# Delta-rule layers: 32 tokens of each of four images to a tile, one state step a tile, four tiles at work, the solution in 32x32 tiles

## The reference

```
q, k = softmax(q), softmax(k); beta = sigmoid(beta)   # from one projection of 776 columns
wk    = W k_t
v_new = beta_t * (v_t - wk)
W     = W + v_new k_t^T
out_t = W q_t
```

## Time and profile before

| | |
|---|---|
| runs | 5322.65, 5342.67, 5358.60 us |
| profiled execution, span | 5373.4 us (its own time; its runs' median is 5342.67) |
| TensorE busy | 4530.5 us, 84% |
| VectorE, ScalarE, GpSimd busy | 2972.1, 2152.0, 831.7 us |
| first delta-rule layer | from 331.4 to 1241.0 us |
| second delta-rule layer | from 1614.2 to 2468.5 us |

### The profile page before, as it was taken

The page is one execution under the profiler, slowest core; times in us unless marked ns, Lnnn a source line. Parts: engine busy times, 40 slices in busy tenths (PEclk is TensorE's granted clock), DMA queues, the critical chain, the costliest instruction groups (busy, mean ns, idle before and its releaser), DMA issues. The chain is left out here.

```text
span 5373.4 us, 139944 instructions
## 1 busy us (share of the span) xinstructions
PE 4530.5 (84%) x57100; PEld 2834.8 (53%) x57101; DVE 2972.1 (55%) x5849; ACT 2152.0 (40%) x4091; POOL 831.7 (15%) x2139
## 2 busy tenths in 40 slices
PE   3679898887997888897688886799999999984995
PEld 1237777773436777774355554354454545433663
DVE  3444444453024544454488886488686877852343
ACT  1133223232123333331466664277575766721221
POOL 0000000000000000000355553011111111104012
PEclk7788878798998988898899998899999999985997
DMA  1000000000000000000100000000000000006123
GB/s 42 2 7 3 3 3 3 3 3 18 0 0 9 4 3 3 3 4 3 38 1 1 1 1 0 10 1 1 1 0 1 0 1 1 0 3 217 61 84 101
DMA packets 47552, 85.70 MB, mean 16 GB/s; under 512 B 7121, under 2 KB 38129, under 8 KB 46065
## 3 DMA queue, kind: packets, MB, share of 16 engines
q1 hardware_dynamic: 40944, 61.84, 3.3%
q0 software_dynamic: 6144, 16.79, 1.0%
HBM read 45.05 MB, written 33.55 MB: 15 GB/s over the span
## 5 line engine op out<-in xcount | busy, mean ns | idle before, releaser
L1775 PE MATMUL psum<-hm_ex,hm_mix 128*128 128x512 f32 x1024 | 510.4, 621 | 42.3 <-ACT hm_Aq L1855 38.3
L1841 ACT ACTIVATE hm_ex<-psum,hm_nm 128x1024 f32<-128x1024 f32 x256 | 285.6, 1116 | 299.4 <-DVE hm_nm L1899 299.4
L1775 PEld LDWEIGHTS psum<-hm_ex,hm_mix 128*128 128x128 f32 x1024 | 175.6, 191 | 352.5 <-issue 344.8
L1914 DVE COPY hm_A<-psum 128x1024 f32<-128x1024 f32 x256 | 312.9, 1222 | 51.5 <-PE psum L1784 47.9
L1909 DVE TENSOR_SCALAR_CACHE_REDUCE hm_plus<-hm_Aq,hm_cbcol,hm_sums 128x1024 f32<-128x1024 f32 x256 | 340.5, 1330 | 0.0
L1899 DVE TENSOR_REDUCE hm_nm<-psum 128x1 f32<-128x1024 f32 x256 | 311.0, 1215 | 13.5 <-PE psum L1763 13.5
L1784 PEld LDWEIGHTS psum<-K,hm_Aq 128*128 128x128 f32 x2048 | 236.6, 140 | 150.0 <-issue 145.4
L957 DVE TENSOR_TENSOR fw_M<-fw_M,psum 128x256 f32<-128x256 f32 x256 | 107.8, 421 | 348.1 <-PE psum L728 345.6
L1846 ACT ACTIVATE hm_junk<-hm_Aq 128x1024 f32<-128x1024 f32 x256 | 270.6, 1057 | 30.3
L1763 PE MATMUL psum<-hm_kt,hm_qd 64*32 64x512 f32 x4096 | 280.1, 606 | 0.0
L1321 ACT ACTIVATE pt_signs<-pt_acts,pt_tb 128x1024 f32<-128x1024 f32 (+1 forms) x224 | 227.6, 1018 | 116.1 <-POOL pt_tb L1188 95.0
(11 more groups left out here) (379 smaller groups left out, 9044.6 us busy)
## 6 DMA issues: line engine op xcount, KB each, us to landing
ex_rows_in<-ex_zero SPq DMA_DIRECT2D x2, 5120.0 KB, 24.8
ex_xs<-ex_rows_in SPq DMA_DIRECT2D x80, 128.0 KB
ex_rows_out<-ex_ys SPq DMA_DIRECT2D x80, 128.0 KB, 1.7
ex_w<-in_ex_w SPq DMA_DIRECT2D x2, 4096.0 KB
X<-in_x SPq DMA_DIRECT2D x2, 2048.0 KB, 12.5
out_y<-X SPq DMA_DIRECT2D x2, 2048.0 KB, 9.0
ff_w<-in_ff_w SPq DMA_DIRECT2D x2, 1024.0 KB, 5.8
pt_w_proc<-in_pt_proc SPq DMA_DIRECT2D x1, 2048.0 KB, 7.6
```

The costliest lines, as they stand in the source:

```text
L1775: mm = pe.matmul(bank[4 + c], mix[:, u, :], ex[:, u, 512 * c:512 * c + 512], start=True, stop=True)
L1841: act.activation(ex[:, u, :], flat2(psum[:, 2 * u:2 * u + 2, :]), ACT.Exp, bias=nm[:, u:u + 1], accum_out=rsum[:, u:u + 1]).then_inc(s_ex, 1)
L1914: dve.tensor_copy(A[:, :, :, QT_ * t:QT_ * t + QT_], flat2(psum[:, 6:8, :]).rearrange("p (m g n) -> p m g n", m=MT, g=HEADS)).then_inc(s_a ...
```

## The change

A tile now holds 32 tokens of each of the four images, one image on each quarter of the partitions. The four groups of a tile belong to different images, so the state is held four times (one per image) and takes one step a tile instead of four; it is set to zero once, not per image. Four tiles are at work: tile i is projected, i-1 factored, i-2 solved, i-3 taken through the state. `solve` uses the compact 32x32 blocks directly, in 4 x 8 small matmuls instead of 8 large ones, so nothing is spread any more. `through_state`, `read_state` and `new_state` (with the part within the group) are made of 32x32 matmuls too. The projection is split into two parts with semaphores of their own. The loop runs seven times. The new order of TensorE and VectorE:

```diff
-    for i in range(-1, 4): ... ; with eng.Fori(1, NT // 4 - 1) ... ; for i in range(NT - 4, NT + 2): ...
+    for i in range(4): ... ; with eng.Fori(1, NT // 4) ... ; for i in range(NT, NT + 3): ...
+    LEN = TILE // B
+    tokens = lambda i: H[...].rearrange("p h (b n) -> p h b n", b=B)[:, :, :, bass.ds(i * LEN, LEN)]
 def solve(by, of, sig):
     for n in range(HEADS):
-        mm = pe.matmul(bank[2][:, 64 * n:64 * n + 64], by[:, n, :], of(n), start=True, stop=True)
+        for b in range(4):
+            mm = pe.matmul(bank[2][rows(b), 64 * n:64 * n + 64], by[rows(b), n, :], of(n)[rows(b)],
+                           start=True, stop=True)
+def read_state(a):
+    for c in range(B):
+        for g in range(2):
+            for j in range(4):
+                at = 256 + 64 * (c // 2) + 32 * g
+                mm = pe.matmul(bank[6 + c % 2][rows(j), at:at + 32], M[rows(j), c % 2, c // 2, g, :],
+                               tr[rows(j), a, 1, g, rows(c)], start=(c < 2 and g == 0), stop=False)
+def through_state(a, half):
+    for g in range(2):
+        for c in range(B):
+            for jb in range(2):
+                j = 2 * half + jb
+                at = 32 * (2 * g + half)
+                mm = pe.matmul(bank[6 + jb][rows(c), at:at + 32],
+                               pkt[rows(j), a % 2, P * g + 32 * c:P * g + 32 * c + 32],
+                               M[rows(j), c % 2, c // 2, g, :], start=True, stop=True)
+def new_state(a, half):
+    for c in (2 * half, 2 * half + 1):
+        for g in range(2):
+            for j in range(4):
+                at = 64 * half + 32 * g
+                n = place(g, j)
+                pe.matmul(bank[6 + c % 2][rows(j), 128 + at:160 + at],
+                          kk[rows(c), a, P * g + 32 * j:P * g + 32 * j + 32], U[rows(c), n, :], ...)
+                mm = pe.matmul(bank[6 + c % 2][rows(j), 256 + at:288 + at], U[rows(c), n, :],
+                               qm[rows(c), a, n, :], ...)
+# TensorE, body i (v = i-1, s = i-2, r = i-3), waits in brackets:
+through_state(r, 0)   [pkt(r), state(r-1), output of r-1 copied]
+solve(nt, first) of s [nt, r0]
+project(i, first 512 columns)
+product(l8, l8t) of v ; through_state(r, 1) ; project(i, the rest)
+product(z1, l2) of v ; solve(nt, later) of s ; read_state(r) [U(r)]
+product(z2, l2) of v ; solve(nt, later) of s ; new_state(r, 0)
+product(tt, l2) of v ; new_state(r, 1) ; turn(i) ; turn_keys(s)
+product(z3, loff) of v ; gram(i, 0) [tr] ; solve(z3, given) of v ; gram(i, 1)
+# VectorE, body i:
+lower(v) ; causal(v) ; solution(s, 0) ; less_max(i) ; corrected(r) ; factor(v, 2) ; sums(i)
+solution(s, 1) ; softmax(i) ; solved(s) ; factor(v, 4) ; state(r)
+# ScalarE, body i:
+l2(v) ; exp(i) ; tt(v) ; tr(i) ; pkt(s) ; output of r [state(r) done] ; nt(v) ; r0(v)
-# gone: keep and the state's reset, spread() for intra, z3x, ntx, inside(), six memsets on GpSimd
...
```

More of the change, by code:

```diff
@@ L618, in fast_weight_stage @@
+        bank, psum = k.bank, k.psum
         rows = lambda c: slice(32 * c, 32 * c + 32)
         flat = lambda ap: ap.rearrange("p h j -> p (h j)")
+        place = lambda g, j: 4 * (j % 2) + 2 * g + j // 2
+        tokens = lambda i: H[:, :, :].rearrange("p h (b n) -> p h b n", b=B)[:, :, :, bass.ds(i * LEN, LEN)]
         def bodies(body, eng, start=None):
-            for i in range(-1, 4):
-                body(i, i % 4, i + 1 < NT, i >= 0, i >= 1, i >= 2)
-            with eng.Fori(1, NT // 4 - 1) as j:
+            for i in range(4):
+                body(i, i, True, i >= 1, i >= 2, i >= 3)
+            with eng.Fori(1, NT // 4) as j:
@@ L631, in bodies @@
                 start()
-            for i in range(NT - 4, NT + 2):
-                body(i, i % 4, i + 1 < NT, i < NT, i - 1 < NT, True)
+            for i in range(NT, NT + 3):
+                body(i, i % 4, False, i < NT + 1, i < NT + 2, True)
         def since(i, n):
@@ L657, in _, with fetch, body @@
[L657 to L661, removed]
+                def fetch(i):
+                    pool.tensor_copy(stage[:, :, :].rearrange("p h (b n) -> p h b n", b=B), tokens(i)).then_inc(s_staged, 1)
+                def body(i, a, new, inv, sol, rec):
+                    if inv:
+                        pool.wait_ge(s_bg, i)
+                        if since(i, 2):
+                            pool.wait_ge(s_t, i * 5 - 5)
+                        pool.tensor_tensor(loff[:, :, :], bg[:, :, :], off, ALU.mult).then_inc(s_lo, 1)
+                    if new and not (isinstance(i, int) and i + 1 >= NT):
+                        pool.wait_ge(s_pj1, i + 1)
+                        fetch(i + 1)
@@ L663, in _, with project @@
+                fetch(0)
+                for i in range(4):
+                    body(i, i, True, i >= 1, i >= 2, i >= 3)
+                with pool.Fori(1, NT // 4 - 1) as j:
+                    for a in range(4):
+                        body(j * 4 + a, a, True, True, True, True)
+                for i in range(NT - 4, NT + 1):
+                    body(i, i % 4, i < NT, True, True, True)
             @block.tensor
             def _(pe):
[L665 to L671, removed]
+                def project(i, n, lo, hi, sig):
+                    for h in range(CH):
+                        mm = pe.matmul(bank[n][:, 0:hi - lo], stage[:, h, :], w[:, h, lo:hi],
+                                       start=(h == 0), stop=(h == CH - 1))
+                    mm.then_inc(sig, 1)
@@ L690, in gram @@
                                 at = 96 * (2 * g + half)
-                                mm = pe.matmul(bank[jb][rows(c), at:at + 96], tr[rows(j), a, 2, g, rows(c)],
+                                mm = pe.matmul(bank[3 + jb][rows(c), at:at + 96], tr[rows(j), a, 2, g, rows(c)],
                                                tr[rows(j), a, :, g, rows(c)], start=True, stop=True)
@@ L719, in with_state @@
[L719 to L743, removed]
+                def read_state(a):
[5 more added lines that the diff above has]
+                                               tr[rows(j), a, 1, g, rows(c)], start=(c < 2 and g == 0), stop=False)
+                    mm.then_inc(s_o, 1)
@@ new lines, in new_state @@
+                def new_state(a, half):
[5 more added lines that the diff above has]
+                                pe.matmul(bank[6 + c % 2][rows(j), 128 + at:160 + at],
+                                          kk[rows(c), a, P * g + 32 * j:P * g + 32 * j + 32], U[rows(c), n, :],
+                                          start=False, stop=False)
+                                mm = pe.matmul(bank[6 + c % 2][rows(j), 256 + at:288 + at], U[rows(c), n, :],
+                                               qm[rows(c), a, n, :], start=False, stop=(half == 1 and g == 1))
+                    mm.then_inc(s_ui, 1)
@@ L747, in body @@
                         pe.wait_ge(s_ptc, r + 1)
-                        pe.wait_ge(s_m, r * 5 + 1)
+                        pe.wait_ge(s_m, r + 1)
+                        if since(i, 4):
+                            pe.wait_ge(s_fin, r)
+                        pe.sem_inc(s_go, 1)
                         through_state(ra, 0)
[L750 to L753, removed]
+                    if sol:
+                        pe.wait_ge(s_nt, s + 1)
+                        pe.wait_ge(s_r0, s + 1)
+                        pe.sem_inc(s_go, 1)
+                        solve(by, first, s_ap)
@@ new lines, in body @@
+                    if new:
+                        pe.wait_ge(s_staged, i + 1)
+                        if since(i, 1):
+                            pe.wait_ge(s_dif, i)
+                        project(i, 0, 0, QKN, s_pj0)
+                    if inv:
+                        pe.wait_ge(s_l8, v + 1)
+                        if since(i, 2):
+                            pe.wait_ge(s_nt, v)
+                        pe.sem_inc(s_go, 1)
+                        product(l8, l8t)
+                    if rec:
+                        pe.wait_ge(s_ra, r * 2 + 1)
+                        pe.sem_inc(s_go, 1)
+                        through_state(ra, 1)
@@ new lines, in body @@
+                    if new:
+                        if since(i, 1):
+                            pe.wait_ge(s_qk, i)
+                        project(i, 1, QKN, 3 * C + HEADS, s_pj1)
+                    if inv:
+                        pe.wait_ge(s_l2, v + 1)
+                        pe.sem_inc(s_go, 1)
+                        product(z1, l2)
+                    if sol:
+                        pe.wait_ge(s_rk, s * 2 + 1)
+                        pe.sem_inc(s_go, 1)
+                        solve(by, later, s_ap)
@@ new lines, in body @@
+                    if rec:
+                        pe.wait_ge(s_u, r + 1)
+                        pe.sem_inc(s_go, 1)
+                        read_state(ra)
+                    if inv:
+                        pe.wait_ge(s_z, v * 2 + 1)
+                        pe.sem_inc(s_go, 1)
+                        product(z2, l2)
```

(61 more changed lines are left out.)

282 lines of the change are left out of this document (92 added, 190 removed).

## The result

The kernel after takes 5503.0 us (median of four runs, 5498.9 to 5506.2) against 5347.3 us of the kernel before on the same chip: a ratio of 1.0306, 95% interval 1.0274 to 1.0338. It is about 3% slower; the forecast was 5445 us.

The account below looks back on a forecast made before the run. Instruction fetch was taken to bound TensorE: 240 packets at 3.7 us (888), plus 25 filling and draining, 20 clock and waits, 933 us a layer; both 1,866 against 1,763.9, 102 more, so 5342.67 becomes 5445 us, range 5230 to 5630.

Parts of the forecast that it names:

- The limit: TensorE in the delta-rule layers: runs dry at the end of each 256-instruction packet, the next being fetched too late.
- F: Theory used in the follow-up runs: instruction packets set the pace, about 4 us each when TensorE runs dry.
- TensorE's own work: Per tile of the two layers: falls from about 22 us to about 16 us at the full clock.
- The number of packets: Per delta-rule layer: 164 instruction packets become 240, as pairs a tile rise from 624 to 912.
- The price of a packet: Layers' instruction fetch: 3.7 us when TensorE runs dry waiting for it, bounds 3.3 and 4.6; 888 us a layer.
- filling, draining, clock and waits: Per layer, beside the packets: 25 us for filling and draining, 20 us for clock and waits.
- The clock: TensorE's granted clock in the layers: low about half the time, 22 us a layer, rounded to 20 with the waits.
- What was costed at nothing: VectorE and ScalarE work beside TensorE's and the GpSimd gather: nothing; weights' DMA at most 1 us; new waits inside the clock term.
- The fetch did not get out of the way: Rival for the layers: the fetch keeps up and TensorE's work decides, 586 us less, 4757 us; chance 0.11.
- The four tiles of a solve: Rival for the 32x32 solve: its tiles, all writing bank 2, run one after another, 6485 us; chance 0.02.
- The cheap packets (3.4 to 3.6): Rival for the layers: the fetch binds at 3.4 to 3.6 us a packet, 5329 us; chance 0.22.
- the dear ones (4.6): Rival for the layers: every dry packet costs the long gap, 4.6 us, 534 us more, 5877 us; chance 0.05.

Follow-up runs that it names:

- e3: Kernel after with every matmul of the five products on 64 columns instead of 32, same number of instructions: 5511.2 us, 1.0318 to the kernel before.
- e4: Kernel after with the last product issued twice, 64 pairs of weight load and matmul more a tile: 5651.3 us, 1.0576 to the kernel before.
- e5: Kernel after with TensorE's loop over the tiles of a layer written out, other engines keeping theirs: 5423.3 us, 1.0150 to the kernel before.
- e6: Kernel before with the state read by two 128x128 matmuls a step instead of eight of 32x32: 5399.3 us, 1.0121 to the kernel before.
- e1: Kernel after with the four solves back to 128x128 matmuls, blocks spread by ScalarE again: 5423.1 us, 1.0129 to the kernel before.
- e2: Kernel before with only the solves changed to 32x32 blocks, no spreading of z3 and nt: 5438.8 us, 1.0168 to the kernel before.
- e7: Kernel before with the state read by two 128x128 matmuls a step and TensorE's loop written out: 5312.3 us, 0.9956 to the kernel before.
- e11: Kernel after with 128x128 solves, products of 64 columns and TensorE's loop written out: 5260.4 us, 0.9887 to the kernel before.
- e9: Kernel before with TensorE's loop over the tiles written out, nothing else: 5264.4 us, 0.9887 to the kernel before.

## Why the prediction was right, and where its size was off

- **The limit.** Right for the kernel after: in it and in e3, e4 and e5, a layer took 3.99 to 4.05 us for each of its packets of 256 instructions, with TensorE busy from 651 to 705 us a layer and the clock from 0.67 to 0.77. For the kernel before the text claimed too much: it took the instructions for its limit as well, and e6, with fewer of them, is slower. The price of a dry packet does not carry over to kernels in which many packets hold large matmuls: by it F missed e1, e2 and e6.
- **TensorE's own work.** The solve was priced at 1.1 us and takes 1.10; through the state at 0.4 and takes 0.36. The gain is there where the clock is full (both rows are at 1.00), and it is worth nothing here.
- **The number of packets.** 240 a layer were forecast, 243 and 237 came.
- **The price of a packet** is the step that was mis-sized. 3.7 us was read from the gap right after a dry place; e4 and e5 give what one more packet costs, (1036.8 - 961.8) / (259 - 240) = 3.95 and (961.8 - 922.0) / (240 - 230) = 3.98 us, on layer means. The median gaps of 3.87 and 3.85 us say the same: the two stretches that I read were a little short. At 3.95, 240 packets are 948 us instead of 888. The other 14 us of a mean layer's 962 stand where I had 45 for filling, draining, clock and waits. TensorE's waits that are not breaks come to 18 and 19 us a layer; of the rest, the clock among it, the sum leaves nothing to pay, so it lies under the fetch. So the two errors were +60 and -31, 29 us a layer, and 2 x 29 = 58 us is what separates 5445 from 5503.
- **The clock.** Expected low half the time, which makes a mean of 0.75; it was 0.69 and 0.71. Its 20 us were not paid: e3 has more clock and the same time.
- **What was costed at nothing** (VectorE, ScalarE, GpSimd, the new waits) cost nothing: 10.4 us of waits for VectorE and ScalarE in the second layer, less than before, and the 7.8 us for the weights' DMA come once a layer.
- **The rivals.** The fetch did not get out of the way: the gaps above stay over 3 us. "Mostly hidden", as the Trainium skill has it (Runtime: NRT & Kernel Launch, Instruction fetch mechanics), does not agree with 272 us of breaks a layer. The four tiles of a solve do run side by side into bank 2: 64 matmuls of 64 columns in 1.10 us, where the four of 264 columns at 2116.79 took 1.16 us, a pace at which 64 x 64 columns would need 4.5 us one after another. That speaks against the Trainium skill (TensorEngine Tiling (Array Packing), Gotcha 1: PSUM Pressure), by which different row tiles can't use one bank at once. The cheap packets (3.4 to 3.6) and the dear ones (4.6) both missed the 3.95.
- **What I did not see:** what a return of the loop costs, 5.7 us in the kernel after. I counted returns in proportion to instructions; they are 80 us of the kernel after and 69 us of the kernel before. In e7 and e11 writing the loop out gave more, 7.2 and 8.9 us a return, for a reason that stays open.

How the clock and the breaks set each other in e1 is not settled: its second layer is slower than its first (951.0 against 904.2 us) with the same instructions, and no run here takes those apart.

## What to carry to other kernels

Before a large matmul is cut into small ones, count the instructions and set 256 of them against the work that they carry: under some 4 us of work per 256, the fetch sets the pace and a shorter matmul gains nothing. A break in the middle of one line, ended by "issue", at equal distances in instructions, is the sign. Where the work is just above that, as in the kernel before (745 and 792 us of TensorE's work in 164 packets, 4.5 and 4.8 us each), a loop written out on TensorE alone, or wider columns at the same count of instructions, are cheap to try: together they gave 2.4% in the kernel before. Where the fetch sets the pace throughout, as in the kernel after, wider columns gave nothing (e3).

## What the runs showed of the hardware

- More TensorE work made a kernel faster: 64 columns for 32 at the same instructions took 65 us off e9, with the mean clock up from 0.87 to 0.95 and 0.96, TensorE's busy time down by 18 us and its breaks by 35 us.
- A return of TensorE's loop cost 5.7 us in the kernel after and 5.8 us in the kernel before: the break there was 3.48 us on the row at 2109.09, against 1.7 to 1.9 us at the three others shown, and with the loop written out a layer needs 6 or 7 (before), 7 or 13 (after) packets less.
- A matmul of 32 columns with 128x128 f32 weights stands in the trace at a mean of 301 ns (e6) against 206 ns with 32x32 weights (before), and the small ones lie side by side: eight small ones for two large ones cost 94 us where the large ones cost 178.
